# Selective scan on one core: five states fed by GpSimd instead of two, three of them behind softplus, with gate projections, turns and tanh reordered

## The reference, cut to what matters

```python
xz = x @ in_proj.T
xh, z = jnp.split(xz, 2, axis=-1)
xc = silu(conv_b + sum(xp[:, k:k + Ls, :] * conv_w[:, k] for k in range(DC)))
dt, Bm, Cm = jnp.split(xc @ x_proj.T, [DR, DR + DS], axis=-1)
delta = softplus(dt @ dt_w.T + dt_b)
A = -jnp.exp(A_log)
h = h * jnp.exp(d_t[:, :, None] * A) + (d_t * u_t)[:, :, None] * B_t[:, None, :]   # over t
y = einsum('bds,bs->bd', h, C_t) + xc * Dsk
return (y * silu(z)) @ out_proj.T
```

## Time and profile before

| | |
|---|---|
| median of 3 runs | 580.38 us (579.7 to 581.75) |
| the profiled execution | 580.82 us, its span 579.1 us |
| ScalarE busy | 444.3 us, 77% |
| TensorE busy | 487.5 us, 84% |
| VectorE busy | 449.7 us, 78% |
| GpSimd busy | 342.7 us, 59% |
| mean granted TensorE clock | 0.956 of full |

### The profile page before, as it was taken

The page is one execution under the profiler, slowest core; times in us unless marked ns, Lnnn a source line. Parts: engine busy times, 40 slices in busy tenths (PEclk is TensorE's granted clock), DMA queues, the critical chain, the costliest instruction groups (busy, mean ns, idle before and its releaser), DMA issues.

```text
span 579.1 us, 9184 instructions
## 1 busy us (share of the span) xinstructions
PE 487.5 (84%) x3346; PEld 401.9 (69%) x3346; DVE 449.7 (78%) x689; ACT 444.3 (77%) x851; POOL 342.7 (59%) x167
## 2 busy tenths in 40 slices
PE   3587999969898999889999968688876587999996
PEld 2245866858786678677965867587765475688696
DVE  5897877849987786898887869769999998777122
ACT  2459888999988799999689999999788641581440
POOL 3103667878969788696897999757577670200000
PEclk9988999979999999999999979999999889997889
DMA  8031121222331222233222222222452213000101
GB/s 264 0 117 38 37 108 67 82 72 80 111 112 50 98 74 74 72 118 111 74 74 72 74 74 99 93 74 74 132 160 74 72 45 138 1 2 1 37 1 37
DMA packets 18237, 44.77 MB, mean 77 GB/s; under 512 B 1360, under 2 KB 7632, under 8 KB 17936
## 3 DMA queue, kind: packets, MB, share of 16 engines
q1 hardware_dynamic: 18192, 44.18, 23.2%
HBM read 42.61 MB, written 1.57 MB: 76 GB/s over the span
## 4 chain that ended last, share of the span: by engine, by line
ACT 37%; PE 36%; DVE 18%; issue 5%; POOL 1%; DMA 1%; POOLq 0%; DVEq 0%; ACTq 0%
ACT dBuT L665 17%; ACT dA L649 11%; PE pro L1319 9%; PE yT L1319 9%; DVE area L1106 8%; PE yT L1323 7%; PE dBu L1323 5%; PE dBu L1319 4%; DVE area L888 1%; PE pro L1323 1%; ACT th L615 1%; ACT area L627 1%; DVE xdbl L1131 1%; ACT pre L624 1%; ACT area L639 1%
## 5 line engine op out<-in xcount | busy, mean ns | idle before, releaser
L557 POOL TENSOR_TENSOR hc<-area 128x1024 f32<-128x1024 f32 x127 | 300.2, 2372 | 124.5 <-DVE area L1103 64.0
L665 ACT ACTIVATE dBuT<-area,bT 128x256 f32<-128x256 f32 x492 | 208.5, 503 | 5.0 <-PE dBu L1323 5.0
L1323 PE MATMUL dBu<-ident,dBuT 128*128 128x128 f32 x992 | 141.5, 282 | 44.8 <-DVE area L1106 22.4
L1323 PEld LDWEIGHTS dBu<-ident,dBuT 128*128 128x128 f32 x992 | 114.5, 144 | 56.4 <-issue 20.2
L649 ACT ACTIVATE dA<-area,Aneg 128x1024 f32<-128x1024 f32 x124 | 141.8, 1147 | 9.1 <-DVE area L1106 9.0
L1323 PE MATMUL yT<-ident,hc 128*128 128x128 f32 x1024 | 138.4, 280 | 1.7 <-POOL hc L557 1.4
L1323 PEld LDWEIGHTS yT<-ident,hc 128*128 128x128 f32 x1024 | 118.5, 144 | 20.4 <-issue 14.7
L1103 DVE TENSOR_TENSOR_SCAN area<-dA,dBu 128x512 f32<-128x512 f32 x62 | 74.7, 1206 | 14.2 <-PE dBu L1323 9.4
L1106 DVE TENSOR_TENSOR_SCAN area<-dA,dBu 128x512 f32<-128x512 f32 x62 | 74.7, 1205 | 11.0 <-PE dBu L1323 7.8
L1103 DVE TENSOR_TENSOR_SCAN area<-dA,area,dBu 128x512 f32<-128x512 f32 x62 | 79.2, 1278 | 4.5 <-DVE area L1103 0.5
L1106 DVE TENSOR_TENSOR_SCAN area<-dA,area,dBu 128x512 f32<-128x512 f32 x62 | 79.2, 1277 | 4.0
(11 more groups left out here) (242 smaller groups left out, 597.9 us busy)
## 6 DMA issues: line engine op xcount, KB each, us to landing
area<-bc_rows SPq DMA_DIRECT2D x64, 512.0 KB, 3.7
dBuT<-w_in SPq DMA_DIRECT2D x1, 2048.0 KB, 9.5
wp<-wpack_in SPq DMA_DIRECT2D x1, 1030.0 KB, 7.2
x<-x_in SPq DMA_DIRECT2D x2, 512.0 KB, 6.4
hc<-bcast_in SPq DMA_DIRECT2D x1, 1024.0 KB, 10.2
Bb<-bc_rows SPq DMA_DIRECT2D x2, 512.0 KB, 3.9
out<-x SPq DMA_DIRECT2D x4, 256.0 KB, 2.4
bc_rows<-xdbl SPq DMA_DIRECT2D x4, 128.0 KB, 3.6
```

The lines of the kernel that those rows point to most:

```text
L557: g_.tensor_tensor(hc[:, e % 3, :], hs[:, e % 3, :], Cb[:, g % 3, :], ALU.mult).then_inc(hc_done, 1)
L665: return nc.scalar.activation(dBuT[:, SCALED.index(g) % 2, n, :], duT[par][:, n, :], ACT.Copy, scale=bT[:, par, n, s:s + 1])
L1323: return nc.tensor.matmul(out, in_, ident[:, :] if idn is None else idn, start=start, stop=True, is_transpose=True, skip_group_check=True)
```

## The change

It makes state 4 of units 0 and 1, state 11 of units 0 and 1, and state 12 of unit 2 direct (state 4 of unit 2 no longer is). States 11, 11 and 12 (`BEHIND`) are the two steps right behind softplus. The inflow goes to buffers that are free at the time (`hold`: delta of the other unit, gz, yg) instead of dA. GpSimd makes each half's product alone, after a chosen step (`PRODUCT_AFTER`). The Z items move behind the DU items; the last Z of unit 2 moves from unit 1 to behind softplus in unit 2; O items of unit 1 come a step later. ScalarE's item comes ahead of the last exp chunk in a direct state's steps, and the item due at the step after next is taken right behind softplus.

```diff
--- before.py
+++ after.py
@@ -45,7 +45,7 @@
 NORM_AT = {9: 0, 10: 1, 24: 5, 25: 6}
-SCALE_AT, GAIN_AT, ADD_AT, LNX_AT = 12, 14, 16, 31
+SCALE_AT, GAIN_AT, ADD_AT, LNX_AT = 12, 15, 18, 31
 POW_AT = (10, 25)
@@ -78,11 +78,12 @@
             steps = [("B", 0, u + 1), ("B", 1, u + 1), ("BT", 0, u + 1)] + [("DT", j, u + 1) for j in range(4)]
             turns = [("DU", j, u + 1) for j in range(4)]
             if u == 0:
-                items = early + [("Z", j, 0) for j in range(4)] + x + steps + [None, None] + z + turns
+                items = (early + [("Z", j, 0) for j in range(4)] + x + steps + [None, None] + z[0:1] + [None, None]
+                         + turns + z[1:4])
             elif u + 2 < NU:
-                items = early + turned + x + steps + added + z + turns
+                items = early + turned + x + steps + [None] + added + [None, None] + turns + z[0:3]
             else:
-                items = early + turned + added + x + steps + [None, None] + turns
+                items = (early + turned + added + x + steps + [None, None] + [("Z", 3, u)] + [None] + turns)
         at = NH * DS * u
         for it in items:
             if it is None:
@@ -110,7 +111,11 @@
 PARTS, ENDS, SP_AT = schedule()
-DIRECT = [DS * u + s for u, s in [(1, 4), (2, 4)]]
+DIRECT_AT = {(0, 4): (1, 3), (0, 11): (8, 10), (1, 4): (1, 3), (1, 11): (8, 10), (2, 12): (10, 12)}
+DIRECT = [DS * u + s for u, s in DIRECT_AT]
+BEHIND = [DS * u + (SP_AT[u] + 3) // NH for u in range(NU - 1)]
+PRODUCT_AFTER = {NH * DS * u + t: (k, half) for k, ((u, s), ts) in enumerate(DIRECT_AT.items()) for half, t in enumerate(ts)}
+ROW_AT = {0: 0, 6: 1, DS: 2, DS + 6: 3, 2 * DS + 5: 4}
 SCALED = [g for g in range(NG) if g not in DIRECT]
 ORDER = [(k, j, 0) for k, j in FIRST_ITEMS]
 ORDER += [it for it in ENDS if it is not None]
@@ -197,6 +202,16 @@
         yg = area3[:, 6:6 + NH, :]
         du = pre
         Bb = sb("Bb", [P, L])
+
+        def hold(g, half):
+
+            u, par = g // DS, g // DS % 2
+            if g not in BEHIND:
+                return delta[1 - par][:, half, :]
+            if u == 1:
+                return gz[0].rearrange("p n d -> p (n d)")[:, half * L:(half + 1) * L]
+            return yg[:, half, :]
+
         wtap = sb("wtap", [P, 2, DC, DI])
         Aneg = sb("Aneg", [P, 2, NH, DS])
         dskip = sb("dskip", [P, 2, NH, P])
@@ -455,12 +470,13 @@
                     wait_item(sp, "LG", 0, 0)
                     for dst, lo, hi in ((w2a, 0, 4), (w2b, 4, 6), (w2c, 6, 8)):
                         sp.dma_start(dst, w2_d[lo:hi].rearrange("e (c p) h -> p e c h", p=P)).then_inc(s_w2, 16)
-                if g + 1 in DIRECT:
-                    k = DIRECT.index(g + 1)
+                sp.dma_start(Cb[:, g % 3, :], crow_d[u, DS + s:DS + s + 1, :].partition_broadcast(P)).then_inc(cb_ready[g % 3], 16)
+                if g in ROW_AT:
+                    k = ROW_AT[g]
+                    row = DIRECT[k] % DS
                     if k:
                         sp.wait_ge(direct_ready, NH * k)
-                    sp.dma_start(Bb[:, :], crow_d[u, s + 1:s + 2, :].partition_broadcast(P)).then_inc(bb_ready, 16)
-                sp.dma_start(Cb[:, g % 3, :], crow_d[u, DS + s:DS + s + 1, :].partition_broadcast(P)).then_inc(cb_ready[g % 3], 16)
+                    sp.dma_start(Bb[:, :], crow_d[u, row:row + 1, :].partition_broadcast(P)).then_inc(bb_ready, 16)
             sp.wait_ge(dbu_ready, dbu_count(NT - 1, NCH - 1))
             sp.dma_start(w1s, w1_d.rearrange("e h f -> h e f")).then_inc(s_w1, 16)
@@ -506,13 +522,16 @@
                 g_.tensor_tensor(du[:, half, :], delta[par][:, half, :], xc[par][:, half, :],
                                  ALU.mult).then_inc(du_ready, 1)
-            def direct_product(e):
-
-                k, half = DIRECT.index(e // NH), e % NH
+            def direct_product(k, half):
+
+                g = DIRECT[k]
                 g_.wait_ge(bb_ready, 16 * (k + 1))
-                g_.wait_ge(du_ready, NH * (e // (DS * NH)) + half + 1)
-                g_.wait_ge(scan_done, NCH * (e - 2))
-                g_.tensor_tensor(dA[:, e % 3, :], du[:, half, :], Bb[:, :], ALU.mult).then_inc(direct_ready, 1)
+                g_.wait_ge(du_ready, NH * (g // DS) + half + 1)
+                if g == BEHIND[1]:
+                    wait_item(g_, "YT", NH * NCH - 1, 0)
+                elif g == BEHIND[2]:
+                    wait_item(g_, "O", NCH - 1, 1)
+                g_.tensor_tensor(hold(g, half), du[:, half, :], Bb[:, :], ALU.mult).then_inc(direct_ready, 1)
             pows = [0]
@@ -547,14 +566,13 @@
                     pool_du(product_at(e), e // (DS * NH) + 1)
                 if e == NT - 1:
                     break
-                if e % NH == 0 and e // NH + 1 in DIRECT:
-                    direct_product(e + NH)
-                    direct_product(e + NH + 1)
                 g_.wait_ge(scan_done, NCH * (e + 1))
                 g_.wait_ge(cb_ready[g % 3], 16 * (g // 3 + 1))
                 if e >= 3:
                     g_.wait_ge(yacc_done, e - 2)
                 g_.tensor_tensor(hc[:, e % 3, :], hs[:, e % 3, :], Cb[:, g % 3, :], ALU.mult).then_inc(hc_done, 1)
+                if e in PRODUCT_AFTER:
+                    direct_product(*PRODUCT_AFTER[e])
                 t2 = e - NH * DS * (NU - 2)
                 if t2 in POW_AT:
                     rstd_pow(0)
@@ -635,6 +653,8 @@
             def softplus(u):
                 _, _, par = unit(u)
                 wait_item(act, "DT", NH * NCH - 1, u)
+                if DIRECT[2 * (u - 1)] not in BEHIND:
+                    act.wait_ge(scan_done, NCH * NH * (DIRECT[2 * (u - 1)] + 1))
                 for half in range(NH):
                     nc.scalar.activation(delta[par][:, half, :], pre[:, half, :], ACT.Softplus).then_inc(delta_ready, 1)
@@ -717,12 +737,22 @@
             scale_blocks(1, 0)
             for e in range(NT):
                 g, half = divmod(e, NH)
-                direct = (e + 1) // NH in DIRECT
                 u, t = divmod(e, DS * NH)
+                direct = (e + 1) // NH in DIRECT and (e + 1) // NH not in BEHIND
                 since = t - SP_AT[u] if u + 1 < NU else -1
+                item = ENDS[e - 1] if e and since != 3 else None
+                item_first = direct or u == NU - 2 and since in (5, 6)
                 if direct:
                     exp_chunk(e + 1, 0)
-                elif e + 1 < NT and since not in (1, 2):
+                if item is not None and item_first:
+                    item_a(*item)
+                if direct:
+                    exp_chunk(e + 1, 1)
+                elif since in (1, 2):
+                    exp_chunk(NH * BEHIND[u] + 1, since - 1)
+                elif since in (3, 4):
+                    exp_tile(e + 2)
+                elif e + 1 < NT and since != 5:
                     exp_tile(e + 1)
                 if since == 0:
                     exp_tile(e + 2)
@@ -730,18 +760,21 @@
                 if half == 0:
                     if g + 1 < NG and g + 1 not in DIRECT:
                         scale_blocks(g + 1, 0 if first else 1)
+                    if since == 1:
+                        scale_blocks(g + 2, 0)
                 else:
                     if first:
                         scale_blocks(g + 1, 1)
-                    if g + 2 < NG and (g + 2) % DS != 0 and g + 2 not in DIRECT:
+                    if g + 2 < NG and (g + 2) % DS != 0 and g + 2 not in DIRECT and since != 2:
                         scale_blocks(g + 2, 0)
-                if direct:
-                    exp_chunk(e + 1, 1)
-                if e and ENDS[e - 1] is not None:
-                    item_a(*ENDS[e - 1])
+                if item is not None and not item_first:
+                    item_a(*item)
                 if since == 0:
                     softplus(u + 1)
-                    exp_tile(e + 3)
+                    if ENDS[e + 2] is not None:
+                        item_a(*ENDS[e + 2])
+                    for i in range(NCH):
+                        exp_chunk(e + 3, i)
                 if e == NH * DS * (NU - 2) + SCALE_AT:
                     first_norm(1, acc, acc).then_inc(first_scaled, 1)
                 elif e == NH * DS * (NU - 2) + LNX_AT:
@@ -1097,7 +1130,7 @@
                 lo, hi = c * CH, (c + 1) * CH
                 decay, inflow = dA[:, e % 3, lo:hi], dBu[q % 3][:, :]
                 if direct:
-                    decay, inflow = inflow, decay
+                    decay, inflow = inflow, hold(e // NH, e % NH)[:, lo:hi]
                 if u % 2 == 0:
                     init = hs[:, e % 3, lo - 1:lo] if i else 0.0
                     nc.vector.tensor_tensor_scan(hs[:, e % 3, lo:hi], decay, inflow, init, ALU.mult, ALU.add).then_inc(scan_done, 1)
```

## The result

The changed kernel takes **585.51 us** (median of 20 runs, 580.86 to 589.07) against 580.96 us for the kernel before (median of 20 on the same chip, 577.44 to 585.51). The ratio is **1.0067, 95% interval 1.0044 to 1.009**: slower by 0.7%, and outside the predicted range of 574.6 to 583.1. The profiled execution took 586.06 us, with a span of 584.3 us (before 579.1).

The account below looks back on a forecast made before the run. No one bottleneck: ScalarE (37%) and TensorE (36%) share the chain. Terms -1.2 + 0 - 1.5 + 0.3 + 2.7 - 2.4 = -2.1 us take 580.82 to 578.7; the median, 0.44 lower, gives 578.3, range 574.6 to 583.1.

Parts of the forecast that it names:

- Front of unit 0: Start of unit 0, bounded by TensorE: without dBu groups for state 4, X2 starts earlier; -1.2 us.
- Rear of unit 0: Unit 0 from the DT items on: step 31's second scan starts at 152.8, before 152.85; 0 us.
- The list of 32.7 us: ScalarE's work in unit 0 from the second table load's end at 118.84 to the last Z tanh at 151.6.
- ScalarE is 2.8 us ahead at its next exp, and nobody needs it: End of unit 0: ScalarE's lead gains nothing, as step 32 and the next X items wait for step 31's scans.
- Front of unit 1: Start of unit 1: the tanh goes ahead of scaling and last chunk, so X2 starts at 182.9, before 184.40; -1.5 us.
- Rear of unit 1: End of unit 1: O items hold step 53's scan, third chunk waits some 0.75 us, one tanh less; +0.3 us.
- Front of unit 2: Start of unit 2: state 4's transposes return, and GpSimd's product ahead of the power delays the first norm; +2.7 us.
- Rear of unit 2: End of unit 2, bounded by ScalarE up to step 97's exp: it gains 2.88, pays 0.48 for a tanh; -2.4 us.
- GpSimd does not end unit 2: Denies a rival: GpSimd's products push hc back, so VectorE ends unit 2 instead of ScalarE; 583.0 us, chance 0.12.
- The clock rival: With fewer transposes behind softplus, TensorE's clock falls to 1.2 GHz, in unit 1 too; sum +2.7, 583.1 us, chance 0.09.

Follow-up runs that it names:

- tanh_between: The changed kernel, but in step 31 of units 0 and 1 ScalarE takes the last tanh between the two groups of four scalings; 579.91 us, ratio 0.9985.
- order_only: The kernel before, with only the Z items of units 0 and 1 moved behind the DU items and no direct state added; 598.06 us, ratio 1.021.
- fill_three: The changed kernel plus transposes of zeros in step 31 of units 0 and 1 and ahead of unit 2's first B item; 579.60 us, ratio 0.9985.
- filled_behind: The changed kernel plus sixteen transposes of zeros in each of the two steps behind softplus of units 0, 1 and 2; 584.42 us, ratio 1.0061.
- power_first: The changed kernel, but at t = 10 of unit 2 GpSimd takes the power ahead of the direct product; 580.72 us, ratio 0.9963.
- state4_too: The changed kernel with state 4 of unit 2 direct again, besides state 12; 586.21 us, ratio 1.0077.
- shifted: The changed kernel with twelve repeated transposes for step 0's first chunk, so all steps start some 2 us later; 585.99 us, ratio 1.0089.
- z_early: The changed kernel with the Z items of units 0 and 1 ahead of the DU items again, direct states kept; 583.42 us, ratio 1.0046.

## Why the prediction was wrong, step by step

- **Front of unit 0, -1.2: right** (-0.96).
- **Rear of unit 0, 0: right, and for the reason given.** The list of 32.7 us put the last tanh in VectorE's way; it started VectorE's multiply at 150.55. With the front's shift of 1.93 taken off, the predicted 152.2 is 150.27, so that is 0.28 late. tanh_between confirms the reason: the tanh moved, the unit ended 1.59 earlier. order_only splits the zero: direct state -2.84 (priced at 2.88), order +3.07.
- **Starts of units 1 and 2: the step that failed.** The sentence "ScalarE is 2.8 us ahead at its next exp, and nobody needs it" looked for who gains from ScalarE's lead, and never asked what TensorE does while VectorE is held; the sum has nothing for it. Each hold of VectorE became 2.01 us of idle TensorE, the X matmuls behind it ran in part at half level, and steps 33 and 65 ended 1.69 and 1.34 us later. That the clock is the cost is shown at both places by the fourteen executions; that it fell behind this idle time is shown at the first, by fill_three beside filled_behind, and argued at the second. That the fall came at all was partly chance: power_first, with the same idle time, had none.
- **Front of unit 1, -1.5: half.** X2 starts 1.41 us behind X1's end (181.54 to 182.95), as worked out. By step 40 the gain was 1.44; 0.8 of it was gone by step 42. The rows say how: the next X item's tanh, which before had waited 1.30 us for TensorE (190.20), now starts at 189.54 right behind an exp and four scalings, with no wait for TensorE, so that ScalarE's list sets it. No run moved it.
- **Rear of unit 1, +0.3: right** as a number (+0.33); its parts were not tested one by one.
- **Front of unit 2, +2.7: too low by 2.4.** The product ahead of the power is 2.08 (2.3 in the sum). Giving up state 4 was put at 0.4 in the sum (and at 0.8 on TensorE, with no reason given for the difference) and is 1.39 (state4_too: 1.43): most of the 1.74 us of transposes arrives, and the cuts for chunks and idle time were guesses. The remaining 1.68 is the clock again, behind an idle stretch that was 0.96 us before and is 3.03 now; in power_first, with the power first, it is 0.95.
- **Rear of unit 2, -2.4: two thirds** (-1.61); 0.48 of the rest is the half clock behind softplus (filled_behind), the other 0.3 is open.
- **Rivals.** GpSimd does not end unit 2: in the changed kernel VectorE waits 2.85 us for an exp ahead of the first scan of unit 3 (375.78), and not for hc. The clock rival was put in the middle of unit 1, where the clock did fall to 0.70 (240 to 245 us) and step 63 does not show it. By the Trainium skill, page "TensorE: Matmul & The Clock Gate", section "What's actually happening", an array that has been idle runs at 1.2 GHz and a busy one at 2.4. The rows agree that half level follows idle time. They also show the same 2.01 us with and without a fall, and, in order_only, 24.00 us of a busy TensorE at half level. A rival that let the clock fall behind any idle stretch of TensorE, and not only in the middle of unit 1, would have been worth far more than 0.09.

Against a sum of -2.1 the steps themselves took 6.27 us longer: 5.71 of the gap of 8.4 stand in the four stretches with a fallen clock, 1.0 in state 4. What the clock fell behind in unit 3 was not tested; no run filled that place.

## What to carry to other kernels

Where a change makes one engine wait for another at a hand-over, write down what TensorE does in that time: an idle stretch of some 2 us can cost as much again behind it, in matmuls that nobody touched. Such a loss comes and goes with the moment at which the stretch falls, so compare step by step, with more than one execution, before a part is given the blame or the credit. And when one side queue serves two masters, put what a long chain waits for (here the power of 1.67 us) ahead of what has steps of time left (the product of 2.35 us).

## What the runs showed of the hardware

- Work that computes nothing can pay: in fill_three sixteen transposes of zeros, 1.91 us of TensorE's time in an idle stretch, kept the next matmuls at 1.89 us, where filled_behind, unfilled at the same time, took 3.37. At all three places 56 transposes took 6.6 us (1.91 twice and 2.78), and the path was 4.7 us shorter, of which only the first 1.69 are sure to be theirs.
- The clock's fall depends on the moment. Behind 2.01 us of idle time at step 31 it fell in the changed kernel, state4_too, filled_behind (matmuls at 154.1 to 154.7 us) and order_only (158.2 us), and stayed up in power_first and shifted (155.6 and 155.9 us). Behind 3.04 us at step 78 it fell in z_early and stayed up in tanh_between, whose matmuls there lie 0.9 us earlier. Which moments are bad was not tried beyond that.
- A busy TensorE is not always back at full level soon: in order_only the granted clock was 0.50 from 523 to 547 us, with TensorE busy all 24.00 us. No run shows why.
